# Newton-Schulz pseudo-inverse: block-diagonal 128x128 operands replaced by pairs of 64x64 products on quarter tiles

## The chip, the cores and the metric

The kernel runs on one core of a Trainium2 chip. The core has five engines that run side by side and meet at semaphores: PE (TensorE, matrix products; its weight loads are shown apart as PEld), DVE (VectorE), ACT (ScalarE), POOL (GpSimd) and SP (SyncE, here only a DMA queue). The metric is the device time of one execution in microseconds.

## What is computed

The input x has 8 batches of 2048 tokens with 256 features. The reference applies two residual blocks. The first is a Nyström attention with 16 heads of 16 features and 64 landmarks a head:

```python
q_l = q.reshape(B, H, M, denom, HS).sum(axis=-2) / denom
k_l = k.reshape(B, H, M, denom, HS).sum(axis=-2) / denom
s1 = jax.nn.softmax(jnp.einsum('bhld,bhmd->bhlm', q, k_l), axis=-1)
s2 = jax.nn.softmax(jnp.einsum('bhmd,bhnd->bhmn', q_l, k_l), axis=-1)
s3 = jax.nn.softmax(jnp.einsum('bhmd,bhld->bhml', q_l, k), axis=-1)
z_star = moore_penrose_pinv(s2, ITERS)
out = s1 @ (z_star @ (s3 @ v))
```

and the pseudo-inverse of each 64x64 matrix s2 is six steps of

```python
z = jnp.swapaxes(x, -1, -2) / (col * row)[..., None, None]
for _ in range(num_iter):
    xz = x @ z
    z = 0.25 * z @ (13.0 * I - xz @ (15.0 * I - xz @ (7.0 * I - xz)))
```

The second block is a gated feed-forward layer with a shift by one token. Both are wrapped in layer norms.

## The kernel before

The program has two parts. **Part 1** makes, for every batch, the layer-norm statistics of all tokens, the landmarks, the matrices s2 and their inverses; it stores landmarks and inverses to DRAM. It takes the eight batches in two groups of four (`for i in range(B // GR)`); the four of a group are called rows, `for s in ROWS`. **Part 2** does everything else, batch by batch, in an order written out by hand (the lists PRO, BODY, LAST); it begins when Part 1 has ended on all engines.

Inside a group of Part 1 each engine's program is a list of steps, and each step runs over the four rows before the next step begins. An engine works strictly in the order of its own program. So when DVE or ACT has a step that takes long, everything behind it in that engine's list waits, even where its operand is ready. The order in a group is: DMA of x1in (three buffers, so the fourth row's load waits until PE has pooled the first row), statistics on DVE (`st`, `mv`, L878 and L883), `pw` (L871), pooling on PE (L1188), landmarks, logits, softmax X (L912 to L926), its transpose XT by PE (L1166), then column sums and the split of XT ("cs, XTlo, XTbd", L945, L931, L940), the scale factor, and the six iterations.

**Numbers.** The products of the inverse are done in f16 with operands split in a high and a low half: a tile with `_d` in its name holds [128 partitions, 8 pairs of heads, 2 halves, 64]. The high half is written by ACT (`high`, L673), the low half by DVE (`low`, L931), both reading the product from PSUM. A product of two split operands takes three matmuls: high x high, high x low, low x high.

**Tiling.** Two heads share the 128 partitions: head 0 of a pair is on partitions 0 to 63, head 1 on 64 to 127. So that one matmul of the full array multiplies both heads without mixing them, the stationary operand is a block-diagonal copy, `_bd`, of [128, 8, 2, 128]: the two heads' 64x64 matrices stand on the diagonal and zeros elsewhere. The zeros are filled in once by POOL at the start of the program (L577, twelve fills). The blocks are copied in by DVE for XT and for S and T3 (`blocks`, L940, two copies a row and step) and by ACT for Z transposed (L687, two copies a row and iteration). `product` (L1172 to L1180) issues the matmuls, all at L1179: for each pair `a` the terms, each with a 128x128 stationary and a 64-column moving operand.

**An iteration.** S = X Z (24 matmuls a row), T2 = 15 I - 7 S + S S (48: the identity and the terms in S go through the array as well, against scaled identities eye15 and eye7), T3 = 13 I - S T2 (32), and last Z' = Z T3 and its transpose (24 each; the last iteration makes the transpose alone). Each of a group's four rows has two PSUM banks, named bank, wide, wide and acc. PE's step for row s waits for DVE's low half (or block copy) of row s; ACT's `high` waits for PE's product, DVE's `low` for ACT's `high`. ACT's copies into ZT_bd stand in its order between the high halves of S and those of T2.

Of the kernel before, what the change touches and what calls it, by code (L numbers as in the profile page):

```python
# [11 lines left out]
P = 128  # L12
# [3 lines left out]
def sandwich(nc, x, Wk, Wq, Wv, Wo, bo, W_r, W_k, W_v, mu_r, mu_k, out):  # L16
# [23 lines left out]
    with ctx:  # L40
# [3 lines left out]
        def sem(name):  # L44
            return ctx.enter_context(nc.semaphore(name))
# [82 lines left out]
        XT_bd = [sb(f"XT_bd{s}", [P, PAIRS, 2, P], F16, c=part1) for s in ROWS]  # L128
        ST_d = [sb(f"ST_d{s}", [P, PAIRS, 2, M], F16, c=part1) for s in ROWS]
        ST_bd = [sb(f"ST_bd{s}", [P, PAIRS, 2, P], F16, c=part1) for s in ROWS]  # L130
        Z_d = [sb(f"Z_d{s}", [P, PAIRS, 2, M], F16, c=part1) for s in ROWS]
        ZT_d = [sb(f"ZT_d{s}", [P, PAIRS, 2, M], F16, c=part1) for s in ROWS]
        ZT_bd = [sb(f"ZT_bd{s}", [P, PAIRS, 2, P], F16, c=part1) for s in ROWS]
# [6 lines left out]
        p_zero = sem("p_zero")  # L140
# [12 lines left out]
                      for s in ROWS for n in names]  # L153
                     + [(n, i, s) for i in range(ITERS) for names in (["S"], ["ZTbd"], ["T2"], ["T3"], ["Z", "ZT"])
                        for s in ROWS for n in names
                        if not (n in ("Z", "ZT", "ZTbd") and i == ITERS - 1)])
# [5 lines left out]
                                           ["max", "shift"], ["sum", "rcp", "X", "rs"], ["cs", "XTlo", "XTbd"],  # L162
                                           ["cm", "cg", "cr", "gb"], ["gcol", "gX", "gXT"], ["Zlo", "ZTlo"])
                      for s in ROWS for n in names]
                     + [(n, i, s) for i in range(ITERS)
                        for names in (["Slo", "Sbd"], ["T2lo"], ["T3lo", "T3bd"], ["Zlo", "ZTlo"])
# [376 lines left out]
        def _(pool):  # L543
# [84 lines left out]
        def _(act):  # L628
# [10 lines left out]
            for i in range(B // GR):  # L639
# [20 lines left out]
                for s in ROWS:  # L660
# [3 lines left out]
                    sc.activation(ST_d[s][:, :, 0, :], XT[s][:, :, :], ACT.Copy, scale=XS).then_inc(p_act, 1)  # L664
# [901 lines left out]
```

## Time and profile before

| | us |
|---|---|
| median of three runs | 2051.49 (2047.1 to 2055.32) |
| the profiled execution | 2045.3 |
| its span, first to last instruction | 2043.6 |
| PE busy | 1669.9 (82%) |
| DVE busy | 1428.1 (70%) |
| ACT busy | 990.2 (48%) |
| POOL busy | 268.8 (13%) |

The mean granted clock of TensorE over the span is 0.93 of its full 2.4 GHz. It has two levels, 1.2 and 2.4 GHz, shown as 0.50 and 1.00. The part of the time that Part 1 takes is read from the timeline: group 1 runs to 281.9 us, group 2 to 534.6. A busy time is an average over parts with different limits, so what a change in one stage is worth has to be read from that stage.

### The profile page before, as it was taken

How to read it: one execution, taken by the hardware profiler on the slowest of the kernel's cores; microseconds unless marked ns; L12 is line 12 of the kernel's file. 1: busy time of each engine (PE TensorE's matmuls, PEld its weight loads, DVE VectorE, ACT ScalarE, POOL GpSimd, SP SyncE). 2: the span in 40 equal slices, each digit the busy share in tenths (PEclk: the TensorE clock that was granted, in tenths of full speed). 3: DMA queues.
4: the chain of work that ended last, by engine and by line, in shares of the span. 5: the costliest groups of instructions: out<-in, count | busy, mean ns of one | idle time of the engine just before them, and what ended most of it. 6: DMA issues, size and time to landing. Idle time of an engine off the chain costs nothing.

```text
span 2043.6 us, 51115 instructions
## 1 busy us (share of the span) xinstructions
PE 1669.9 (82%) x21644; PEld 1141.4 (56%) x21644; DVE 1428.1 (70%) x3036; ACT 990.2 (48%) x1615; POOL 268.8 (13%) x134
## 2 busy tenths in 40 slices
PE   2758767687477988998898899889889988988885
PEld 1557755577345545655654655465456556556554
DVE  8487784877773688379468837956883794788265
ACT  1147721577223544654554465355446535543652
POOL 4000000000300111112111101211111121112022
PEclk9869988699787999999999999999999999999997
DMA  5230001000122121212212121221213122221110
GB/s 162 74 103 3 4 22 52 2 3 3 54 50 53 46 63 42 84 38 52 76 46 62 42 80 42 52 75 47 63 41 94 27 52 76 64 53 39 43 32 31
DMA packets 125700, 104.66 MB, mean 51 GB/s; under 512 B 30368, under 2 KB 123424, under 8 KB 125472
## 3 DMA queue, kind: packets, MB, share of 16 engines
q1 hardware_dynamic: 124320, 99.29, 17.8%
q8 instruction: 172, 2.82, 0.6%
q10 hardware_dynamic: 1152, 2.10, 0.3%
q14 instruction: 56, 0.46, 0.1%
HBM read 56.23 MB, written 19.92 MB: 37 GB/s over the span
## 4 chain that ended last, share of the span: by engine, by line
PE 49%; DVE 30%; issue 10%; ACT 8%; POOL 2%; DMA 1%; DVEq 0%; POOLq 0%; ACTq 0%; SPq 0%
PE bank L1491 5%; PE bank L1283 4%; DVE m L1035 4%; ACT ZT_bd L687 4%; PE bank L1470 4%; PE acc L1366 4%; PE bank L1511 3%; PE bank L1294 3%; PE acc L1283 3%; PE bank L1533 3%; DVE m L1027 3%; PE wide L1388 3%; DVE ST_d L931 2%; DVE ST_bd L940 2%; PE wide L1451 2%
## 5 line engine op out<-in xcount | busy, mean ns | idle before, releaser
L605 POOL TENSOR_TENSOR xm<-yy,xres 128x1024 f32<-128x1024 f32 x32 | 91.8, 2869 | 591.9 <-issue 339.3
L772 ACT ACTIVATE p<-wide 128x1024 f32<-128x1024 f32 x128 | 123.9, 1020 | 78.7 <-PE wide L1451 78.7
L743 ACT ACTIVATE e<-wide 128x1024 f32<-128x1024 f32 x128 | 130.0, 1022 | 63.9 <-PE wide L1388 58.9
L1035 DVE TENSOR_REDUCE m<-wide 128x16 f32<-128x1024 f32 x128 | 149.8, 1212 | 15.6 <-PE wide L1330 15.6
L1027 DVE TENSOR_REDUCE m<-wide 128x2 f32<-128x1024 f32 x128 | 149.3, 1215 | 10.0 <-PE wide L1310 10.0
L1533 PE MATMUL bank<-wvT,ka 128*128 128x256 f32 x512 | 133.7, 420 | 4.9 <-ACT ka L818 4.3
L1511 PE MATMUL bank<-wrT,xrT 128*128 128x256 f32 x512 | 124.3, 398 | 11.0 <-DVE ob L1121 6.4
L1491 PE MATMUL bank<-wo,oT 128*128 128x256 f32 x512 | 120.1, 388 | 4.5 <-DVE oT L1070 2.6
L621 POOL TENSOR_TENSOR ob<-ob,xm 128x1024 f32<-128x1024 f32 x32 | 76.5, 2390 | 355.7 <-DVE ob L273 355.7
L1533 PEld LDWEIGHTS bank<-wvT,ka 128*128 128x128 f32 x512 | 105.4, 211 | 30.2 <-issue 8.2
L1511 PEld LDWEIGHTS bank<-wrT,xrT 128*128 128x128 f32 x512 | 98.6, 198 | 31.1 <-issue 10.3
L1491 PEld LDWEIGHTS bank<-wo,oT 128*128 128x128 f32 x512 | 96.0, 192 | 27.2 <-issue 12.2
L1283 PE MATMUL bank<-xT,w 128*128 128x512 f16 x384 | 97.0, 406 | 7.7 <-DVE xT L1008 4.8
L1521 PE MATMUL acc<-xkT,wkT 128*128 128x512 f32 x192 | 88.3, 603 | 16.2 <-DVE oT L1070 16.2
L615 POOL TENSOR_TENSOR xkT<-x2T 128x1024 f32<-128x1024 f32 x32 | 60.6, 1892 | 309.8 <-ACT x2T L797 309.8
L1057 DVE RECIPROCAL rr<-bank 128x4 f32<-128x4 f32 x16 | 2.8, 183 | 138.6 <-PE bank L1401 138.5
L1294 PE MATMUL bank<-w,xT 128*128 128x256 f16 x768 | 89.2, 273 | 12.6 <-DVE ql L1016 12.6
L1366 PE MATMUL acc<-e,vv 128*17 128x64 f32 x4096 | 85.0, 223 | 16.8 <-issue 8.4
L1470 PE MATMUL bank<-p,ones_pair 128*32 128x512 f32 x512 | 85.5, 651 | 10.0 <-ACT p L772 10.0
L1294 PEld LDWEIGHTS bank<-w,xT 128*128 128x128 f16 x768 | 74.3, 98 | 30.3 <-DVE ql L1016 18.1
L1283 PE MATMUL acc<-xT,w 128*128 128x512 f16 x384 | 88.8, 381 | 0.0
L940 DVE COPY ST_bd<-ST_d 64x1024 f16<-64x1024 f16 x192 | 80.9, 422 | 11.1
(285 smaller groups left out, 3916.6 us busy)
## 6 DMA issues: line engine op xcount, KB each, us to landing
x1in<-in_L_attn_x SPq DMA_DIRECT2D x8, 2048.0 KB, 13.6
xin<-in_L_attn_x SPq DMA_DIRECT2D x32, 512.0 KB, 4.9
k_stack<-kh SPq DMA_DIRECT2D x256, 64.0 KB, 2.2
xres<-in_L_attn_x SPq DMA_DIRECT2D x32, 512.0 KB, 4.4
out<-ob SPq DMA_DIRECT2D x32, 512.0 KB, 2.9
k_stack<-kl SPq DMA_DIRECT2D x128, 64.0 KB, 2.0
q_stack<-landmarks SPq DMA_DIRECT2D x192, 4.0 KB, 1.6
inverse<-X ACTq DMA_DIRECT2D x8, 256.0 KB, 2.2
```

Source lines behind the costliest of these rows:

```text
L743: sc.activation(e3[t % 2][:, :], wide[t % 2][:, :], ACT.Exp).then_inc(wide_drained[t % 2], 1)
L772: sc.activation(p1[:, 2 * j:2 * j + 2, :], wide[w][:, :].rearrange("p (a n) -> p a n", a=2), ACT.Exp).then_inc(wide_drained[w], 1)
L940: ins = v.tensor_copy(dst[r, :, :, j * M:(j + 1) * M], src[r, :, :, :])
L1027: v.tensor_reduce(m3[:, 2 * j:2 * j + 2, c], wide[j % 2][:, :].rearrange("p (a n) -> p a n", a=2), AX.X, ALU.max).then_inc(wide_drained[j ...
L1035: v.tensor_reduce(m1[:, tiles, 2 * w:2 * w + 2, :].rearrange("p t q x -> p q t x"), wide[w][:, :].rearrange("p (q t x m) -> p q t x m", q= ...
L1283: ins = mm(dst[o][:, :], w16[:, w, wt, k, o * P:(o + 1) * P], xT[:, xt, k, :], start=(i == 0), stop=(i == len(TERMS) - 1))
L1294: ins = mm(bank[j][:, t * A:(t + 1) * A], xT[:, xt, k, tok], w16[:, 2, wt, k, :], start=(i == 0), stop=(i == len(TERMS) - 1))
L1366: ins = mm(acc[k][32 * q:32 * q + HS + 1, j * M:(j + 1) * M], vv[:, t, h, :], e3[t % 2][:, h * M:(h + 1) * M], start=(first and j == 0), s ...
L1470: s_ = mm(bank[k][r, :], ones_pair[:, :], p1[:, a, :], start=True, stop=True)
L1491: ins = mm(dst, oT[:, k, tok], wo[:, k, :], start=(k == 0), stop=(k == KB - 1))
L1511: ins = mm(bank[j][:, t * A:(t + 1) * A], xrT[:, k, tok], wrT[:, k, :], start=(k == 0), stop=(k == KB - 1))
L1533: ins = mm(bank[j][:, t * A:(t + 1) * A], ka[:, k, tok], wvT[:, k, :], start=(k == 0), stop=(k == KB - 1))
```

## The change

Each head's product is done by itself on a quarter of the array: the stationary and the moving operand are 64 partitions x 64 columns, rows 0 to 63 go to the upper left quarter and rows 64 to 127 to the lower right one, and the two quarters alternate, term by term. The operands are now the `_d` tiles themselves. The tiles XT_bd, ST_bd and ZT_bd, the copies into them on DVE and ACT, and POOL's fills are gone. Since S must now outlive the making of T2 (it is read as an operand from its `_d` tile), T2 gets a tile of its own, T2_d, and XT gets XT_d instead of a turn in ST_d. PE's two waits for the end of ACT and DVE between Part 1 and Part 2 are gone too.

```diff
             def product(dst, left, right, added=()):
 
+                halves = [slice(j * HALF, (j + 1) * HALF) for j in range(2)]
                 for a in range(PAIRS):
-                    terms = [(scaled(a), identity) for scaled, identity in added]
-                    terms += [(left[:, a, 0, :], right[:, a, 0, :]), (left[:, a, 0, :], right[:, a, 1, :]),
-                              (left[:, a, 1, :], right[:, a, 0, :])]
-                    for n, (l, r) in enumerate(terms):
-                        ins = mm(dst[:, a * M:(a + 1) * M], l, r, start=(n == 0), stop=(n == len(terms) - 1))
+                    terms = [[(scaled(r, a), identity[r, :]) for scaled, identity in added]
+                             + [(left[r, a, 0, :], right[r, a, 0, :]), (left[r, a, 0, :], right[r, a, 1, :]),
+                                (left[r, a, 1, :], right[r, a, 0, :])] for r in halves]
+                    last = len(terms[0]) - 1
+                    for n in range(last + 1):
+                        for j, r in enumerate(halves):
+                            ins = mm(dst[r, a * M:(a + 1) * M], *terms[j][n], start=(n == 0), stop=(n == last))
                 return ins
...
-            for s in ROWS:
-                for t in (XT_bd, ST_bd, ZT_bd):
-                    g.memset(t[s][:, :, :, :], 0.0).then_inc(p_zero, 1)
...
-                    if it < ITERS - 1:
-                        for s in ROWS:
-                            if it == 0:
-                                act.wait_ge(p_dve, of(dve_steps, i, "ZTlo", s))
-                            else:
-                                act.wait_ge(p_dve, of(dve_steps, i, "ZTlo", it - 1, s))
-                            act.wait_ge(p_zero, 3 * GR)
-                            for j in range(2):
-                                r = slice(j * HALF, (j + 1) * HALF)
-                                ins = sc.activation(ZT_bd[s][r, :, :, j * M:(j + 1) * M], ZT_d[s][r, :, :, :], ACT.Copy)
-                            ins.then_inc(p_act, 1)
                     for s in ROWS:
-                        high("T2", it, s, ST_d, pb[s][1], -1.0 / SS)
+                        high("T2", it, s, T2_d, pb[s][1], -1.0 / SS)
...
-                    low(("XThi", s), ST_d[s], XT[s][:, :, :], XS)
-                    blocks(("XTlo", s), XT_bd[s], ST_d[s])
+                    low(("XThi", s), XT_d[s], XT[s][:, :, :], XS)
...
                         low(("S", it, s), ST_d[s], pm(pb[s][0]), SS / (XS * ZS))
-                        blocks(("Slo", it, s), ST_bd[s], ST_d[s])
                     for s in ROWS:
-                        low(("T2", it, s), ST_d[s], pm(pb[s][1]), -1.0 / SS)
+                        low(("T2", it, s), T2_d[s], pm(pb[s][1]), -1.0 / SS)
                     for s in ROWS:
                         low(("T3", it, s), ST_d[s], pm(pb[s][0]), 1.0 / SS)
-                        blocks(("T3lo", it, s), ST_bd[s], ST_d[s])
...
-            pe.wait_ge(p_act, len(act_steps) * B // GR)
-            pe.wait_ge(p_dve, len(dve_steps) * B // GR)
```

The order on PE, where the first iteration of a group begins (S of the four rows, then T2 of row 0's first pair). Before:

```order
L1179 MATMUL bank0<-Z_d0,XT_bd0 128x64 x24
L1179 MATMUL wide0<-Z_d1,XT_bd1 128x64 x24
L1179 MATMUL wide1<-Z_d2,XT_bd2 128x64 x24
L1179 MATMUL acc0<-Z_d3,XT_bd3 128x64 x24
L1179 MATMUL bank1<-eye15,ident16 128x64
L1179 MATMUL bank1<-eye7,ST_bd0 128x64 x2
L1179 MATMUL bank1<-ST_d0,ST_bd0 128x64 x3
```

and after:

```order
L1153 MATMUL bank0<-Z_d0,XT_d0 64x64 x48
L1153 MATMUL wide0<-Z_d1,XT_d1 64x64 x48
L1153 MATMUL wide1<-Z_d2,XT_d2 64x64 x48
L1153 MATMUL acc0<-Z_d3,XT_d3 64x64 x48
L1153 MATMUL bank1<-eye15,ident16 64x64 x2
L1153 MATMUL bank1<-eye7,ST_d0 64x64 x4
L1153 MATMUL bank1<-ST_d0 64x64 x6
```

The steps stand in the same order; each has twice the matmuls of half the height.

The order on ACT in an iteration, from the high halves of S on. Before:

```order
L673 ACTIVATE ST_d<-bank 128x8x64
L673 ACTIVATE ST_d<-wide 128x8x64 x2
L673 ACTIVATE ST_d<-acc 128x8x64
L687 ACTIVATE ZT_bd<-ZT_d 64x16x64 x8
L673 ACTIVATE ST_d<-bank 128x8x64
L673 ACTIVATE ST_d<-wide 128x8x64 x2
L673 ACTIVATE ST_d<-acc 128x8x64
```

and after:

```order
L667 ACTIVATE ST_d<-bank 128x8x64
L667 ACTIVATE ST_d<-wide 128x8x64 x2
L667 ACTIVATE ST_d<-acc 128x8x64
L667 ACTIVATE T_d<-bank 128x8x64
L667 ACTIVATE T_d<-wide 128x8x64 x2
L667 ACTIVATE T_d<-acc 128x8x64
```

The eight copies between S and T2 are gone, and T2's halves go to their own tile (T_d is T2_d with its number left out).

The order on DVE for the low halves of S, after the eight pieces of Z and ZT. Before:

```order
L931 SCALAR_TENSOR_TENSOR ST_d<-bank,ST_d 128x8x64
L940 COPY ST_bd<-ST_d 64x16x64 x2
L931 SCALAR_TENSOR_TENSOR ST_d<-wide,ST_d 128x8x64
L940 COPY ST_bd<-ST_d 64x16x64 x2
L931 SCALAR_TENSOR_TENSOR ST_d<-wide,ST_d 128x8x64
L940 COPY ST_bd<-ST_d 64x16x64 x2
L931 SCALAR_TENSOR_TENSOR ST_d<-acc,ST_d 128x8x64
L940 COPY ST_bd<-ST_d 64x16x64 x2
```

and after, with the first of T2's:

```order
L914 SCALAR_TENSOR_TENSOR ST_d<-bank,ST_d 128x8x64
L914 SCALAR_TENSOR_TENSOR ST_d<-wide,ST_d 128x8x64 x2
L914 SCALAR_TENSOR_TENSOR ST_d<-acc,ST_d 128x8x64
L914 SCALAR_TENSOR_TENSOR T_d<-bank,T_d 128x8x64
L914 SCALAR_TENSOR_TENSOR T_d<-wide,T_d 128x8x64 x2
```

The copies of T3 and of XT go in the same way.

## Rows read from the trace of the kernel before

**Rows 1.** The page: the chain that ended last, by engine and line.

```profile
PE bank L1491 5%; PE bank L1283 4%; DVE m L1035 4%; ACT ZT_bd L687 4%; PE bank L1470 4%; PE acc L1366 4%; PE bank L1511 3%; PE bank L1294 3%; PE acc L1283 3%; PE bank L1533 3%; DVE m L1027 3%; PE wide L1388 3%; DVE ST_d L931 2%; DVE ST_bd L940 2%; PE wide L1451 2%
```

**Rows 2.** Windows, both groups' iterations: length, PE, PEld, DVE, ACT, POOL busy (count), clock.

```profile
130.20:282.00 151.80, 120.01 (x3552) 114.48 (x3552) 120.58 (x223) 109.00 (x155) 0.00 (x0) 0.93 0.02 6
383.60:534.70 151.10, 119.97 (x3552) 114.37 (x3552) 119.83 (x221) 108.48 (x154) 0.00 (x0) 0.93 0.02 6
```

**Rows 3.** The chain of waits from 172 to 199, by line.

```profile
by line: ACT ZT_bd L687 31.4%; PE wide L1179 12.2%; DVE ST_d L931 10.1%; DVE Z_d L931 9.2%; DVE ZT_d L931 8.8%; PE bank L1179 8.5%; DVE ST_bd L940 6.3%; issue 6.0%; ACT ST_d L673 4.5%; PE acc L1179 3.9%; ACT Z_d L673 2.2%; DVEq L862 0.2%
```

**Rows 4.** Timeline of DVE and ACT, 182 to 199: start, us, instruction, [idle before].

```profile
182.13 0.69 DVE L931 SCALAR_TENSOR_TENSOR Z_d<-bank,Z_d 128x512 f16<-128x512 f32 x1
182.74 0.68 DVE L931 SCALAR_TENSOR_TENSOR ZT_d<-bank,ZT_d 128x512 f16<-128x512 f32 x1
...
188.60 8.56 ACT L687 ACTIVATE ZT_bd<-ZT_d 64x1024 f16<-64x1024 f16 x8
...
197.81 0.69 DVE L931 SCALAR_TENSOR_TENSOR ST_d<-bank,ST_d 128x512 f16<-128x512 f32 x1 [4.20 <-ACT ST_d L673]
```

**Rows 5.** Timeline of PE, warm and cold, and the window of the cold one.

```profile
179.61 0.86 PE L1179 MATMUL bank<-ZT_d,ST_bd 128*128 128x64 f16 x24
...
133.47 2.75 PE L1179 MATMUL wide<-Z_d,XT_bd 128*128 128x64 f16 x48
...
134.00:137.00 3.00, 3.00 (x61) 3.00 (x59) 2.88 (x6) 1.49 (x3) 0.00 (x0) 0.50 0.02 5
```

**Rows 6.** Timeline of PE on f32 operands (stationary size first), and windows there.

```profile
107.30 1.97 PE L1166 MATMUL wide<-ident,X 64*64 64x64 f32 x32 [0.30 <-DVE X L922]
...
1023.73 3.19 PE L1417 MATMUL bank<-un,zt 64*64 64x16 f32 x32
...
92.96 1.95 PE L1209 MATMUL bank<-qlT,qbd 128*128 128x64 f32 x16
...
52.55 7.07 PE L1188 MATMUL wide<-x1in,pw 128*64 128x256 f32 x32
...
107.30:109.30 2.00, 1.97 (x32) 1.78 (x32) 1.93 (x4) 0.96 (x2) 0.00 (x0) 0.50 1.09 348
1023.70:1027.00 3.30, 3.30 (x40) 3.22 (x40) 1.33 (x5) 2.13 (x4) 0.00 (x0) 0.50 0.08 11
92.00:96.00 4.00, 4.00 (x39) 4.00 (x37) 1.62 (x4) 1.13 (x4) 0.00 (x0) 1.00 0.19 61
```

**Rows 7.** Timeline, first and last pieces around group 1's iterations.

```profile
130.86 0.68 DVE L931 SCALAR_TENSOR_TENSOR Z_d<-XT,Z_d 128x512 f16<-128x512 f32 x1
...
281.24 0.68 DVE L985 TENSOR_SCALAR X<-acc 128x512 f32<-128x512 f32 x1
```

**Rows 8.** Timeline of DVE, one row of "cs, XTlo, XTbd" to the next.

```profile
112.34 0.68 DVE L945 TENSOR_REDUCE rc<-XT 128x8 f32<-128x512 f32 x1
...
114.61 0.69 DVE L945 TENSOR_REDUCE rc<-XT 128x8 f32<-128x512 f32 x1
```

**Rows 9.** Timeline of POOL, DVE and ACT at the start, and a window.

```profile
3.47 1.80 POOL L577 MEMSET XT_bd<- 128x2048 f16 x1
...
3.56 21.00 DVE L841 CAST ident<-ident 128x128 f16<-128x128 f32 x1 [3.56 <-POOL eye L573]
...
25.25 0.68 DVE L854 SCALAR_TENSOR_TENSOR w<-wq,w 128x512 f16<-128x512 f32 x1
...
29.45 5.32 DVE L878 BATCH_NORM_STATS2 st<-x1in 128x6 f32<-128x256 f32 x16
...
15.72 0.62 ACT L638 ACTIVATE w<-wq 128x512 f16<-128x512 f32 x1
...
30.00:35.00 5.00, 0.00 (x0) 0.00 (x0) 4.86 (x16) 0.00 (x0) 0.00 (x0) 1.00 0.00 0
```

**Rows 10.** Timeline of PE in Part 2 and its window.

```profile
651.04 0.64 PE L1366 MATMUL acc<-e,vv 128*17 128x64 f32 x32
...
650.00:652.00 2.00, 2.00 (x79) 1.63 (x72) 0.00 (x0) 1.90 (x2) 0.00 (x0) 1.00 0.03 8
```

More of the change, by code:

```diff
@@ L127, in sandwich @@
         XS, ZS, SS = 64.0, 16.0, 16.0
-        XT_bd = [sb(f"XT_bd{s}", [P, PAIRS, 2, P], F16, c=part1) for s in ROWS]
+        XT_d = [sb(f"XT_d{s}", [P, PAIRS, 2, M], F16, c=part1) for s in ROWS]
         ST_d = [sb(f"ST_d{s}", [P, PAIRS, 2, M], F16, c=part1) for s in ROWS]
-        ST_bd = [sb(f"ST_bd{s}", [P, PAIRS, 2, P], F16, c=part1) for s in ROWS]
+        T2_d = [sb(f"T2_d{s}", [P, PAIRS, 2, M], F16, c=part1) for s in ROWS]
         Z_d = [sb(f"Z_d{s}", [P, PAIRS, 2, M], F16, c=part1) for s in ROWS]
         ZT_d = [sb(f"ZT_d{s}", [P, PAIRS, 2, M], F16, c=part1) for s in ROWS]
-        ZT_bd = [sb(f"ZT_bd{s}", [P, PAIRS, 2, P], F16, c=part1) for s in ROWS]
         pb = [[bank[0][:, :], bank[1][:, :]], [wide[0][:, 0:512], wide[0][:, 512:1024]],
@@ L153, in sandwich @@
                       for s in ROWS for n in names]
-                     + [(n, i, s) for i in range(ITERS) for names in (["S"], ["ZTbd"], ["T2"], ["T3"], ["Z", "ZT"])
+                     + [(n, i, s) for i in range(ITERS) for names in (["S"], ["T2"], ["T3"], ["Z", "ZT"])
                         for s in ROWS for n in names
-                        if not (n in ("Z", "ZT", "ZTbd") and i == ITERS - 1)])
+                        if not (n in ("Z", "ZT") and i == ITERS - 1)])
         STATS = ([("st", 0), ("st", 1)] + [k for s in range(2, GR) for k in (("pw", s - 2), ("st", s))]
@@ L161, in sandwich @@
                      + [(n, s) for names in (["stl", "mvl", "xl"], ["lmlo", "qbd"],
-                                           ["max", "shift"], ["sum", "rcp", "X", "rs"], ["cs", "XTlo", "XTbd"],
+                                           ["max", "shift"], ["sum", "rcp", "X", "rs"], ["cs", "XTlo"],
                                            ["cm", "cg", "cr", "gb"], ["gcol", "gX", "gXT"], ["Zlo", "ZTlo"])
@@ L932, in low @@
                                            op0=ALU.mult, op1=ALU.subtract).then_inc(p_dve, 1)
-                def blocks(lo_key, dst, src):
-                    dve.wait_ge(p_zero, 3 * GR)
-                    done(*lo_key)
-                    for j in range(2):
-                        r = slice(j * HALF, (j + 1) * HALF)
-                        ins = v.tensor_copy(dst[r, :, :, j * M:(j + 1) * M], src[r, :, :, :])
-                    ins.then_inc(p_dve, 1)
                 for s in ROWS:
@@ L1230, in _ @@
                         pe.wait_ge(p_dve, of(dve_steps, i, *key))
-                        product(pb[s][0], XT_bd[s], Z_d[s]).then_inc(p_pe, 1)
+                        product(pb[s][0], XT_d[s], Z_d[s]).then_inc(p_pe, 1)
                     for s in ROWS:
-                        pe.wait_ge(p_dve, of(dve_steps, i, "Sbd", it, s))
-                        product(pb[s][1], ST_bd[s], ST_d[s],
-                                [(lambda a: ident16[:, :], eye15[:, :]),
-                                 (lambda a: ST_bd[s][:, a, 0, :], eye7[:, :]),
-                                 (lambda a: ST_bd[s][:, a, 1, :], eye7[:, :])]).then_inc(p_pe, 1)
+                        pe.wait_ge(p_dve, of(dve_steps, i, "Slo", it, s))
+                        S_ = ST_d[s]
+                        product(pb[s][1], S_, S_, [(lambda r, a: ident16[r, r], eye15),
+                                                   (lambda r, a: S_[r, a, 0, :], eye7),
+                                                   (lambda r, a: S_[r, a, 1, :], eye7)]).then_inc(p_pe, 1)
                     for s in ROWS:
                         pe.wait_ge(p_dve, of(dve_steps, i, "T2lo", it, s))
-                        product(pb[s][0], ST_bd[s], ST_d[s],
-                                [(lambda a: ident16[:, :], eye13[:, :])]).then_inc(p_pe, 1)
+                        product(pb[s][0], ST_d[s], T2_d[s], [(lambda r, a: ident16[r, r], eye13)]).then_inc(p_pe, 1)
                     for s in ROWS:
-                        pe.wait_ge(p_dve, of(dve_steps, i, "T3bd", it, s))
+                        pe.wait_ge(p_dve, of(dve_steps, i, "T3lo", it, s))
                         if it < ITERS - 1:
-                            pe.wait_ge(p_act, of(act_steps, i, "ZTbd", it, s))
-                            product(pb[s][1], ZT_bd[s], ST_d[s]).then_inc(p_pe, 1)
-                        product(pb[s][0], ST_bd[s], ZT_d[s]).then_inc(p_pe, 1)
-            pe.wait_ge(p_act, len(act_steps) * B // GR)
-            pe.wait_ge(p_dve, len(dve_steps) * B // GR)
+                            product(pb[s][1], ZT_d[s], ST_d[s]).then_inc(p_pe, 1)
+                        product(pb[s][0], ST_d[s], ZT_d[s]).then_inc(p_pe, 1)
             pe.wait_ge(w16_lo, 3)
```

5 lines of the change are left out of this document (2 added, 3 removed).

## The prediction

> **What bounds the kernel now.** I read the page's chain of waits first: PE's lines lead it, but DVE's and ACT's block-diagonal copies stand among its largest entries, DVE ST_bd and ACT ZT_bd [rows 1]. All of them lie in two stretches, the six iterations of the inverse for batches 0 to 3 and for 4 to 7, so I read those alone: 151.8 and 151.1 us, with PE, DVE and ACT each busy for 109 to 120 us of them [rows 2]. No engine is full; the stage goes in turns. The chain of one iteration says whose turn is longest: ACT's copies into ZT_bd hold 31% of it, DVE's into ST_bd 6% [rows 3]. The timeline shows how: ACT starts eight copies at 188.60 and works on them for 8.56 us. The evacuation of T2 stands behind them in ACT's order, so DVE has nothing to read until 197.81, after 4.20 us of idleness [rows 4]. PE waits behind DVE. A full iteration comes to about 25 us, a sixth of the stage.
>
> The stage's work on PE is 3552 products a group: a row of the batch needs 24 (XZ) + 48 (T2) + 32 (T3) + 24 + 24 (Z and its transpose) = 152, four rows 608, five iterations of that, and a last one without Z of 512; the count in the windows agrees [rows 2]. A product is one load and one matmul of 64 columns. 24 of them take 0.86 us, of which the last one's own latency is 0.193, so one starts every 29.0 to 29.2 ns while the clock is at the upper level, 2.4 GHz; at the lower level, 1.2 GHz, 48 take 2.75 us, 53 ns each [rows 5]. 3552 x 0.0292 = 103.7 us: that is the floor under the stage's 151, and 47 us are turns.
>
> **The change, part by part.**
>
> *Copies of ACT and DVE.* Gone are 40 ACT copies a group, and 48 pairs of DVE copies of 0.86 us inside the iterations. What stays of each engine in a full iteration is 20 evacuations at 0.60 us pitch (the pitch of DVE's pieces in [rows 4]; ACT's pieces are as long), 12 us for either. PE's part is above 17, so PE becomes the bound if its turns close. They do: after XZ of the last row the first T2 needs one ACT and one DVE piece, 1.5 us with latencies, while PE still has three rows of XZ, 3 x 0.7 us; DVE's eight Z pieces, 4.8 us, fit under PE's Z and ZT products, 5.6 us. Every later step has longer rows and the same two pieces. So the stage is PE's product count times the pace of a quarter-tile pair.
>
> *The pace of a pair.* Each product becomes two, one in the upper left and one in the lower right quarter, each with its own load of 64 columns. The instructions double to 7104 loads and 7104 matmuls a group. Are two quarters worked on at once? The trace has both cases, with f32 operands. The transposes of X alternate the two quarters: 32 matmuls in 1.97 us, of which 0.31 is latency, 53.5 ns each at the lower clock. The product of un and zt walks through one quarter first and then the other: 32 in 3.19 us at the same clock, 94 ns each, with the same load of 64 columns and a shorter matmul [rows 6]. A load in one quarter and one in the other thus run side by side, and a pair of the first kind takes 107 ns, the time of one load.
>
> What does a load of 64 f16 columns take at the upper clock? For f32, 128 columns are loaded in 111.7 ns ((1.95 - 0.275)/15), with matmuls of 64 columns behind them that would need only 54 by the 216 ns of 256 columns ((7.07 - 0.38)/31). So the load sets this pace: 106.7 ns, two cycles a column, and 5 on top [rows 6]. f16 matmul columns cost half of f32 ones: 29.2 for 64 against 216 for 256. I take the same half for the load: 64 columns in 26.7 ns, and with the 5 on top a pair every 31.7 ns. Bounds: from below the 29.2 of today (a matmul of 64 columns cannot stream faster); from above the load at f32's two cycles, 53.3 + 5 = 58.3 ns. I stand near the lower end because the rows show that the matmul side halves, and the load is the same stream of columns.
>
> The Trainium skill speaks against this change here: "TensorEngine Tiling (Array Packing)", section Restrictions, says that column tiling disables Fast Weight Load. The 128-column f16 loads have it, the 64-column ones would not. "TensorE: Matmul & The Clock Gate", section LDWEIGHTS, gives such a load as its columns over 1.2, which is 53.3 ns for 64; by that estimate the pair would take 53 to 58 ns and the sum would be that of the first rival. The trace's f32 loads agree with this formula (106.7 for 128); for f16 no row shows it.
>
> Sum of the stage: 3552 x 0.0317 = 112.6 us. In front stand 1.3 us (DVE's first two pieces from 130.86 on [rows 7], 0.60 + 0.68). The clock is at the lower level until about 137 [rows 5]: 5 us in which 94 pairs pass instead of 158, 2.0 us lost. Behind the last product stands one DVE piece, 0.8 us. Together 116.7, against 281.92 - 130.86 = 151.1 now [rows 7]. That saves 34.4 a group, **68.8 us** for two. PE then has no idle stretch in the stage, so I count no second fall of the clock.
>
> *Copies into XT_bd.* A row of "cs, XTlo, XTbd" takes DVE 2.27 us (112.34 to 114.61) on the chain, of which 0.60 + 0.60 remain [rows 8]. 4 rows x 1.07 x 2 groups = **8.6 us**. ACT's pieces for the last row do not take their place: the transposes of row 1 start at 107.30 [rows 6], those of row 3 two turns of 2.27 later, at 111.8, and with 2.0 for them and 0.6 + 0.6 for ACT are over at 115.1; DVE's new pace gets to that row at 115.9. Bounds: 7 if ACT's last piece holds DVE a little, 9 if not.
>
> *The fills on POOL.* Twelve fills of 1.80 us run from 3.47 on. DVE's cast of ident, 128 columns, is issued at 3.56 and lasts 21.00 us, until the last fill is over [rows 9], where 512 columns take DVE 0.69 [rows 4]. Without the fills DVE is through with its constants by 6 at the latest and waits for ACT's f16 weights, which start at 15.72 and give the first at 16.4. From the first weight piece (25.25) to the first statistics (29.45) are 4.2 us, so these start at 20.6: **8.8 us** sooner. x1in is no new wait: the three first loads are all in before 30, as the window with no traffic shows, and DVE now reaches the third at 33.8. Pooling, the fourth load and all that follows hang on this chain. Bounds 0 (should the cast wait for something else) and 9.
>
> The Trainium skill gives the reason for the long cast ("SBUF — State Buffer", Who interferes with whom): a DVE copy or cast in a two-port mode and a GpSimd instruction exclude each other. By it the cast is short again once the fills are gone; the trace agrees, with 21.00 us beside them.
>
> *The rest.* PE's final waits on ACT and DVE go: its next instruction waits for xhat from DVE, which itself waits for both, nothing. T2_d costs nothing; each evacuation writes as many bytes as before. Part 2 is only moved earlier.
>
> Sum: 68.8 + 8.6 + 8.8 = 86.2. The profiled execution took 2045.3 us (span 2043.6) and would take 1959. The median of the runs is 2051.5, 6 above it; from there I predict **1965 us**. A measurement of this kernel can tell some 0.5%, 10 us, from no change.
>
> **The rivals.**
>
> *Slow loads (slower than before).* The f16 load of 64 columns goes at f32's pace, 58.3 ns a pair: 3552 x 0.0583 = 207.1, 94.5 more than in my sum, 189 for two groups: 2154 us. For it: no row shows an f16 load under 128 columns. Against: the halving above. It turns from gain to loss at 31.7 + 86.2/(2 x 3.552) = 43.8 ns a pair.
>
> *Lower clock (slower).* Half of the array stands still in these matmuls, and the chip might grant only 1.2 GHz: 53.3 ns a pair, 189.3 a group, 74.7 more after the 2.0 already counted, 2115 us. Against: around 651, with 17-column matmuls for half of the time, the clock stays at 1.00 [rows 10].
>
> *Delivery.* PE must take four instructions per pair, one every 7.9 ns, for 100 us without a pause. Bursts do it: 32 matmuls and 32 loads in 0.64 us of which 0.22 is latency, 6.8 ns an instruction [rows 10]. Over longer stretches the trace shows less: 79 + 72 in 2.00 us in the same place, 13 ns each, which the work there sets. At 10 ns an instruction a pair takes 40: 142.1 a group, 2 x 29.5 more, 2024 us, still a gain.
>
> *It does not do what it says:* quarters taken one after the other, 63 ns a pair, over 2180. The transposes speak against it.
>
> **How the numbers follow.** My forecast 0.72, delivery 0.06, slow loads 0.14, lower clock 0.06, the rest 0.02. The forecast's own range: 29.2 instead of 31.7 ns takes 18 off, an earlier rise of the clock 4 and the spread of the runs 4, 1940; 36 ns adds 31 and a lost start 9, 2005. To hold 8 in 10 the range takes in delivery and ends at 2030. Faster: forecast and delivery, 0.78; within 0.5%: 0.02; slower: slow loads, clock and the rest, 0.20.
>
> **What the profile after would show.** Each group's stage at some 117 us with PE busy nearly throughout; the products of a row of Z, 48 matmuls now, in 0.76 us plus latency (0.70 at 29.2, 1.4 for the rival); DVE and ACT idle for a third of an iteration; the granted clock at 1.00 from the first iteration on; DVE's cast at 3.6 lasting under 1 us and the first statistics at 20.6. I am wrong if the pair takes over 36 ns, if the clock falls inside the stage, or if PE shows waits between the steps.

## The result and the profile after

The changed kernel takes **2134.9 us** (median of 4 runs, 2131.9 to 2140.3) against 2049.3 for the kernel before in the same runs: 1.042 of its time, with a 95% interval of 1.038 to 1.046. I had predicted 1965, with a range of 1940 to 2030. The change is a loss of 4%, where I forecast a gain of 4%.

The page of the profiled execution (2140.3 us, span 2138.5) already names what is new. These are its two lines on the chain that ended last, by engine and by line:

```profile
PE 57%; DVE 20%; issue 15%; ACT 3%; POOL 2%; DMA 1%; SPq 0%; POOLq 0%; DVEq 0%; ACTq 0%
PE wide L1153 6%; PE bank L1459 4%; PE bank L1251 4%; DVE m L1006 3%; PE bank L1438 3%; PE acc L1334 3%; PE bank L1501 3%; PE bank L1479 3%; PE bank L1262 3%; PE acc L1153 3%; PE bank L1153 3%; PE acc L1251 3%; PE wide L1356 3%; DVE m L998 3%; PE wide L1419 2%
```

ACT's ZT_bd and DVE's ST_bd [rows 1] are gone from it, as they should be. In their place stands "issue", 15% of the span where it had 10: time in which an engine waits for nothing that the profile shows. Where it lies, the windows of the two groups' iterations tell, the rows that answer to [rows 2] (length, then PE, PEld, DVE, ACT, POOL busy and count, then granted clock, DMA share, GB/s):

```profile
117.50:321.00 203.50, 131.44 (x7104) 125.32 (x7104) 82.75 (x121) 66.86 (x112) 0.00 (x0) 0.94 0.03 7
418.20:621.90 203.70, 129.80 (x7104) 124.10 (x7104) 82.61 (x121) 66.86 (x112) 0.00 (x0) 0.95 0.02 6
```

From its first product to its last a group took 147.9 us before and takes 203.5 now. DVE fell from 120 to 83 us of work and ACT from 109 to 67, and the clock is at 0.94. PE is busy for 131 of 203.5 us: it is neither full nor, as before, waiting for a copy. The chain in the middle of the stage, 164 to 175.4, shows what it does in the other 72 (its line by line, then start, us, what):

```profile
by line: issue 43.6%; PE acc L1153 20.8%; PE bank L1153 19.6%; PE wide L1153 19.4%
...
163.74 1.24 issue
164.98 1.36 PE acc L1153 x74
166.34 0.85 PE bank L1153 x54
167.19 1.24 issue
168.44 0.34 PE bank L1153 x10
168.78 1.87 PE wide L1153 x118
170.65 1.24 issue
```

No other engine is on this chain, nor on that of the whole stage from 118 to 320, where "issue" is 72 us:

```profile
by line: issue 35.5%; PE wide L1153 32.5%; PE acc L1153 16.7%; PE bank L1153 15.4%
```

PE works for 2.2 us, stands still for 1.24, works again, in a period of 3.45 us. Between two idle pieces stand 74 + 54 = 128 matmuls, and then 10 + 118 = 128 again: with their loads, 256 instructions. And while it works it is as fast as forecast: 118 matmuls in 1.87 us, 15.8 ns each, 31.7 for a pair of quarters. The transfers of the stage carry the other half of the explanation. These are the rows of queue 8, which brings instructions (packets, MB, share of 16 engines), of the changed kernel from 118 to 320, and of the kernel before from 130 to 282:

```profile
q8 instruction: 55, 0.90, 1.8%
```

```profile
q8 instruction: 28, 0.46, 1.3%
```

55 packets of 16 KB in 202 us, one every 3.67 us, for 14208 loads and matmuls a group: 258 to a packet. PE's instructions arrive in blocks of some 256, and it uses a block up in 2.2 us where the next comes 3.45 to 3.7 us after the last. The kernel before took 28 blocks in 152 us, one every 5.4.

The start and end of each packet, as the trace records them, fit the pauses. Packets end at 163.76, 167.09, 170.40 and 173.81, and PE goes on at 164.98, 168.44, 171.89 and 175.34, each time 1.2 to 1.5 us after one is in. In none of the traces of this case do two packets of queue 8 start less than 3.2 us apart.

The kernel before, which has no product of this kind, shows such a pause too. In Part 2 its packets start at 1361.74, 1365.15 and 1368.69 and the next only at 1374.56; that one ends at 1375.49. PE goes on at 1377.00. Its chain from 1373 to 1381 has this piece:

```profile
1375.31 1.69 issue
```

So such a pause comes without quarter tiles. Whether it is what sets the length of the stage, the experiments ask.

### The profile page after: what moved, and what is told of

Its sections match the earlier page's. It is cut to its first block, busy times and chain, and to the rows that moved or that the text cites. A ratio compares the mean times of both kernels' runs of the same rounds, so it can differ in the third digit from the quotient of the medians.

```text
span 2138.5 us, 64838 instructions
## 1 busy us (share of the span) xinstructions
PE 1693.1 (79%) x28748; PEld 1161.2 (54%) x28748; DVE 1329.2 (62%) x2828; ACT 908.9 (42%) x1535; POOL 247.8 (12%) x122
## 4 chain that ended last, share of the span: by engine, by line
PE 57%; DVE 20%; issue 15%; ACT 3%; POOL 2%; DMA 1%; SPq 0%; POOLq 0%; DVEq 0%; ACTq 0%
PE wide L1153 6%; PE bank L1459 4%; PE bank L1251 4%; DVE m L1006 3%; PE bank L1438 3%; PE acc L1334 3%; PE bank L1501 3%; PE bank L1479 3%; PE bank L1262 3%; PE acc L1153 3%; PE bank L1153 3%; PE acc L1251 3%; PE wide L1356 3%; DVE m L998 3%; PE wide L1419 2%
## 5 line engine op out<-in xcount | busy, mean ns | idle before, releaser
L1041 DVE TENSOR_TENSOR oT<-acc,oT 128x512 f32<-128x512 f32 x64 | 42.3, 681 | 67.8 <-ACT oT L766 67.7
```

## The experiments

Two theories. **Supply:** PE's instructions come in at no more than 256 per 3.45 to 3.7 us, some 14 ns each, and the stage lasts as long as its instructions take to arrive, whatever the array does. **Quarters:** the stalls belong to the work on quarter tiles itself, and 128 such matmuls cost one.

### Fewer instructions, the same array work

```diff
+                if whole is not None:
+                    mm(dst.rearrange("p (a m) -> p a m", m=M), ident16[:, :],
+                       whole[:, :].unsqueeze(1).to_broadcast([P, PAIRS, M]), start=True, stop=False)
...
-                        product(pb[s][0], ST_d[s], T2_d[s], [(lambda r, a: ident16[r, r], eye13)]).then_inc(p_pe, 1)
+                        product(pb[s][0], ST_d[s], T2_d[s], (), eye13).then_inc(p_pe, 1)
```

> The changed kernel, with one edit: the identity term of T2 and of T3 (16 times the identity against 15 or 13 times it), eight pairs of quarter-tile products a row, becomes one product of the whole array with 512 columns. The array gets about the same work (8 pairs at 32 ns = 256 ns before, one of 512 columns at some 216 ns now), but 30 instructions fewer for each such step, 60 a row and iteration: 14208 PE loads and matmuls a group become 12768. Theory 1 (PE's instructions arrive at no more than one per 14.3 ns, 256 every 3.67 us): the stage falls with the count, 204 to 183 us a group, 41 us for both, to about 2094 us. Theory 2 (the stalls belong to the quarter tiles or to the pace of the array): at most the 2 x 48 x 0.04 = 4 us of array time go, about 2131 us.

Measured: 2104.6 us, 1.025 of before (1.021 to 1.029), 30 less than the changed kernel. The first group's window:

```profile
117.00:297.00 180.00, 133.25 (x6384) 115.49 (x6384) 83.11 (x122) 67.03 (x113) 0.00 (x0) 0.97 0.03 8
```

179.6 us from first to last product, 24 less. The second group took 187.5; the stages of 14208 instructions vary as much between groups and kernels, 196 to 206 us. Per instruction that is 179.6 / 12768 = 14.1 ns, against 203.5 / 14208 = 14.3. The array's busy time rose by 2 us while the stage fell by 24: this is supply's answer. The 4 us that I expected of the other theory were too few by its own terms: 768 quarter matmuls fewer a group are also six stalls fewer, some 8 us a group, so it asked for about 2115 us and a stage near 194. The run is outside that too. The time in which PE stood still fell from 72 to 46 us in the group, where six stalls are 8. The control is the same edit on the kernel before:

> The kernel before, with the identity terms of T2 and of T3 as one product of 512 columns each: 28 instructions fewer a row and iteration, the array's work the same to within 2%. It is the control of the same edit on the changed kernel, which gained 24 us in the first group. Theory 1 (instruction supply bounds only a stage that asks for more than 256 in 3.67 us): before, the products take 29.2 ns, 128 of them 3.74 us, so supply does not bound and the groups stay at 147.9 us from first to last product, the time within 0.3%. If the edit itself is cheaper for the array, the groups fall here as well, by up to 24 us each.

Measured: 2051.6 us, 1.001 (0.999 to 1.003), and a group as long as before, 148.3 us from first to last product:

```profile
130.00:279.00 149.00, 121.06 (x3216) 108.36 (x3216) 117.45 (x217) 107.80 (x153) 0.00 (x0) 0.92 0.01 3
```

The edit is worth nothing where supply doesn't bind.

### Less array work, the same instructions

```diff
-                            ins = mm(dst[r, a * M:(a + 1) * M], *terms[j][n], start=(n == 0), stop=(n == last))
+                            l, m = terms[j][n]
+                            ins = mm(dst[j * HALF:j * HALF + 32, a * M:a * M + 32], l[:, 0:32], m[:, 0:32],
+                                     start=(n == 0), stop=(n == last))
```

> The changed kernel with every product of the iterations cut to 32 of its 64 output rows and 32 of its 64 columns, the rest of each inverse left out: a load of 32 columns and a matmul of 32 columns in place of 64 and 64, so the array has half the work per instruction, and the instructions are as many as before, 14208 a group. Theory 1 (supply: 256 instructions in 3.67 us): nothing is gained, 204 us a group, 2135 us in all, with the runs between the idle pieces shorter and the idle pieces longer. Theory 2 (the array's pace on quarters): a pair takes about 16 to 20 ns in place of 32, and the stage falls towards the 12 us an iteration that the evacuations need, under 120 us a group, below 1970 us.

Measured: 2134.9 us, the changed kernel's time to the tenth. Its window, the chain from 160 to 182 by line, and queue 8 from 118 to 314:

```profile
118.00:314.00 196.00, 104.82 (x7094) 98.73 (x7095) 80.74 (x122) 66.96 (x113) 0.00 (x0) 0.51 0.03 8
```

```profile
by line: issue 45.2%; PE wide L1154 33.0%; PE bank L1154 11.3%; PE acc L1154 10.5%
```

```profile
q8 instruction: 55, 0.90, 1.9%
```

The array has half the columns to load and half to stream, PE's busy time falls by 27 us, and the stage by 7. (Even that 7 need not be the edit's: the stage of the changed kernel itself, unedited but for fills on POOL, took 199.5 and 197.8 us in the run with the fills put back, below.) Even the clock doesn't matter: it is granted at 0.51 here, the lower level, against 0.94, and the time is the same. The idle pieces are longer, 1.57 to 1.84 us, where PE needs less for a block; stalls of a fixed length would have made the stage 105 + 72 = 177 us. Again 55 blocks of instructions, now in 196 us. This is the cleanest of the runs: the array is not what the stage waits for.

### Two runs meant for the same question that answered another

A kernel with one quarter alone:

```diff
-                        for j, r in enumerate(halves):
+                        for j, r in list(enumerate(halves))[:1]:
```

> The changed kernel with the lower right quarter of every product of the iterations left out, so half of the heads get no inverse: 7104 loads and matmuls a group instead of 14208, all in one quarter, so nothing of them runs side by side. Theory 1 (instruction supply): a load and matmul in one and the same quarter come every 31.7 ns by my forecast, slower than the supply's 2 x 14.3 = 28.6 ns, so the long idle pieces of PE put down to issue vanish, and each group takes about 117 us: 2049 - 14.7 x 2 (what the changed kernel gains in front of the iterations is 14.7 and 5) ... in short about 1963 us. Theory 2 (a stall of 1.2 to 1.8 us belongs to every 128 quarter matmuls): 28 stalls of 1.4 us stay in each group, about 155 us, 2040 us in all. A quarter's load taking 53 ns would show as a pitch of 58 ns and 207 us a group.

Measured: 2113.5 us, 1.029 (1.024 to 1.034). Its window, and two pieces of its chain:

```profile
116.00:306.00 190.00, 189.65 (x3552) 189.51 (x3552) 83.14 (x123) 67.06 (x113) 0.00 (x0) 0.50 0.02 5
```

```profile
139.95 1.28 PE bank L1153 x24
141.23 5.12 PE wide L1153 x96
```

The stalls are gone, as supply has it: 128 matmuls take 6.8 us here and the next block is in long before. The other theory wanted 28 stalls in 3552 quarter matmuls, and no two instructions of PE start more than 0.06 us apart in the 190. But both theories missed the time, since neither reckoned with the clock: PE is busy for all of the 190 us, and the granted clock stays at 0.50, 1.2 GHz. A matmul comes every 5.12 / 96 = 53.3 ns. 3552 x 0.0533 = 189.4 is the whole group. My rival "lower clock" had this number for the full kernel; it holds for a single quarter alone.

Waits added on PE in the kernel before:

```diff
                     for n, (l, r) in enumerate(terms):
+                        pe.wait_ge(eyes_made, 4)
+                        pe.wait_ge(const_made, NCONST)
```

> The kernel before, with its full-array products and its copies, and two more wait instructions on PE ahead of each product's load, on conditions long met: 4 instructions per product, 14208 a group, as many as the changed kernel has, and the array's work is unchanged. Theory 1 (instruction supply): each group's iterations go from 151 to about 204 us, idle pieces put down to issue come up in them about every 64 products, and the whole takes about 2156 us. Theory 2 (the stalls belong to quarter tiles): the waits cost at most the few ns that PE's sequencer needs for each, hidden under the 29 ns of a product, and the time stays within 1% of the kernel before.

Measured: 2695.4 us, 1.31. Neither expectation, 2156 us or within 1%, came near: a wait on a condition long met isn't free on PE. A row of the timeline, and the window from 140 to 250:

```profile
140.63 1.56 PE L1181 MATMUL acc<-Z_d,XT_bd 128*128 128x64 f16 x11
```

```profile
140.00:250.00 110.00, 109.21 (x828) 85.89 (x827) 25.73 (x45) 31.71 (x41) 0.00 (x0) 0.50 0.01 1
```

828 products in 110 us, 133 ns each, where 53 is the pace of a product at this same lower clock: two waits cost some 80 ns, and no idle piece comes up. The instructions don't come thick enough to ask anything of the supply, so this run tells nothing between the theories.

### The order of the quarters

```diff
-                    for n in range(last + 1):
-                        for j, r in enumerate(halves):
+                    for j, r in enumerate(halves):
+                        for n in range(last + 1):
```

> The changed kernel, each pair's terms ordered otherwise: all terms of the upper left quarter, then all of the lower right one. Same instructions, same count. Theory 1 (instruction supply, and a load is hidden only under a matmul of the other quarter): products of one quarter come every 31.7 ns, 128 of them take 4.06 us, more than the 3.67 us in which 256 instructions arrive, so the idle pieces put down to issue nearly vanish and PE's own pace sets the stage: 7104 x 0.0317 = 225 us plus 4, 24 more than the changed kernel a group, 2183 us. If the order of the quarters does not matter to the array, the pitch stays at 16 ns and the time at 2135 us. Theory 2 (stalls belong to the quarters): both add up, 225 + 55 stalls of 1.4 us, over 2300 us.

Measured: 2141.6 us, 1.043 (1.038 to 1.048), the same as the changed kernel. Its window shows the same stalls, and the same pace between them:

```profile
117.00:321.00 204.00, 127.58 (x7100) 122.08 (x7094) 82.90 (x122) 66.86 (x112) 0.00 (x0) 0.97 0.03 8
```

The times of the two theories, 2183 us and over 2300, didn't come; what did is the case that the expectation had set beside them, in which the order doesn't matter to the array. Three to six terms of one quarter in a row are no slower than quarters in turn, so the run tells nothing between the theories. It looks as if PE begins work of the other quarter from several instructions ahead; that is my interpretation, no row shows it. Whether there is an end to it, the next kernel asks, with 24 to 48 of one quarter in a row:

```diff
-                for a in range(PAIRS):
+                for j in range(2):
+                    r = slice(j * HALF, (j + 1) * HALF)
+                    for a in range(PAIRS):
```

> The changed kernel, each product of a row ordered otherwise: all eight pairs of the upper left quarter (24 to 48 matmuls in a row), then all eight of the lower right one. Same instructions, 14208 a group. With three to six of a quarter in a row the stage took 203.7 us and a matmul came every 16 ns between the idle pieces, as with quarters in turn. Theory A (work of the two quarters runs side by side only as far as the engine looks ahead, and 24 are beyond that): each comes every 31.7 ns at the upper clock, 128 in 4.06 us against 3.67 us of supply, so 7104 x 0.0317 = 225 us a group and 2183 us in all; and should one quarter at a time keep the clock at its lower level, as in the kernel with one quarter alone, 53.3 ns each, 379 us a group and 2490 us in all. Theory B (the load and the matmul of one quarter overlap enough for 16 ns by themselves): supply stays the bound, 204 us a group and 2135 us in all.

Measured: 2404.9 us, 1.175 (1.170 to 1.179). The first group's window:

```profile
116.00:452.00 336.00, 333.12 (x7048) 333.12 (x7049) 85.15 (x126) 69.16 (x116) 0.00 (x0) 0.50 0.01 3
```

336 us a group with PE busy throughout and the clock at 0.50 to the end. It is theory A in its second form, a little better than its 379: 336 / 7104 = 47.3 ns a matmul, where 53.3 is the pace of one quarter at this clock, and the start times show where the difference lies: 53 to 54 ns apart inside one quarter's run, 26 to 28 for a few where the other quarter's begins. The order matters after all once the runs are long. How much of the 132 us is the order's and how much the clock's this run doesn't separate. The clock alone is not enough: in the changed kernel quarters in turn came every 26.7 ns at the lower clock (48 in 1.49 us, of which 0.24 is the last one's latency), and 7104 x 0.0267 = 190 us would still lie under the supply's 204.

```profile
117.50 1.49 PE L1153 MATMUL bank<-Z_d,XT_d 64*64 64x64 f16 x48 [6.22 <-DVE ZT_d L914]
```

### The fills at the start

```diff
+            for s in ROWS:
+                for t in range(3):
+                    if t:
+                        pool.wait_ge(p_zero, 3 * s + t)
+                    g.memset(filled[s][:, :, :, :], 0.0).then_inc(p_zero, 1)
```

> The changed kernel with twelve fills of 1.80 us put back on POOL at the place where they stood, into tiles that nothing reads. If the fills were what held DVE's first cast, the cast lasts 21 us again and the first statistics start at 29.4 in place of 20.14 us: 9.3 us slower, 2144 us. If the cast waited for something else that the change took away, the time stays at 2135 us.

Measured: 2134.4 us (1.036 to 1.046 of before). The 9.3 us didn't come, because the long cast didn't: the first statistics start at 19.83 here. So the run doesn't price the late start that it was made for. Yet the fills do hold the cast; it is the waits between them, needed because three fills now share one tile, that let it through. The cast and the first fills of this run; then the same cast where 8 fills follow each other without a wait (the kernel of the next section), and in the changed kernel without fills:

```profile
3.48 5.53 POOL L579 MEMSET filled<- 128x2048 f16 x3
3.57 1.79 DVE L832 CAST ident<-ident 128x128 f16<-128x128 f32 x1 [3.57 <-POOL eye L573]
```

```profile
3.56 14.01 DVE L829 CAST ident<-ident 128x128 f16<-128x128 f32 x1 [3.56 <-POOL eye L572]
```

```profile
3.56 0.23 DVE L824 CAST ident<-ident 128x128 f16<-128x128 f32 x1 [3.56 <-POOL eye L571]
...
20.14 5.33 DVE L861 BATCH_NORM_STATS2 st<-x1in 128x6 f32<-128x256 f32 x16
```

21.00 us behind 12 fills without waits [rows 9], 14.01 behind 8, 1.79 behind one, 0.23 with none: the cast waits for the fills that POOL starts back to back, 1.75 us each, and gets in at the first pause.

### Quarter tiles for one product only

Supply says where quarter tiles should pay: where they take a copy off the path, and the stage's instructions stay within what arrives. Of the three copies ACT's into ZT_bd is the dearest, 31% of the chain [rows 3], and the product that it serves is 24 of a row's 152.

```diff
-                            pe.wait_ge(p_act, of(act_steps, i, "ZTbd", it, s))
-                            product(pb[s][1], ZT_bd[s], ST_d[s]).then_inc(p_pe, 1)
+                            quarters(pb[s][1], ZT_d[s], ST_d[s]).then_inc(p_pe, 1)
```

Only PE's part is shown. ACT's copies into ZT_bd and POOL's four fills of it are gone as well.

> The kernel before, where only the product with ZT on its left (24 of 152 products of a row) goes to quarter tiles, which makes ACT's copies into ZT_bd and their fills needless; the copies into ST_bd and XT_bd stay. 2 x 24 instructions more for each row: 1408 for each of the first five iterations in place of 1216. Theory 1 (supply): 1408 instructions arrive in 20.2 us, about what DVE (20 pieces of 0.60 and 8 pairs of 0.86, 19 us) and PE (17.7 and a little) need, so an iteration falls from 25 to some 21 us and a group from 151 to about 131; with a start 6.6 us earlier (8 fills in place of 12 keep DVE's cast) this is 2050 - 40 - 7 = 2003 us. Theory 2 (quarter tiles carry the stalls, 1.4 us for each 128 matmuls): 192 quarter matmuls an iteration add 2.1 us, some 2023 us. A kernel faster than both would be the outcome of either.

Measured: **1997.9 us**, 0.976 of the kernel before (0.973 to 0.979), faster than both. Its two groups, and its chain from 160 to 200:

```profile
124.00:252.20 128.20, 117.77 (x4032) 111.75 (x4032) 117.41 (x217) 66.91 (x113) 0.00 (x0) 0.98 0.02 4
356.00:484.20 128.20, 118.11 (x4032) 111.98 (x4032) 117.40 (x217) 66.88 (x113) 0.00 (x0) 0.98 0.02 4
```

```profile
by line: DVE ST_bd L928 29.6%; DVE ST_d L919 22.8%; DVE Z_d L919 12.4%; DVE ZT_d L919 12.0%; PE acc L1167 11.7%; ACT ST_d L672 4.5%; issue 4.5%; PE bank L1167 2.4%; DVEq L850 0.7%
```

128 us a group, 3 under what was expected, with DVE and PE busy for 117 each. 8064 instructions at 14.3 ns are 115 us: supply is just inside, "issue" is 4.5%, and the chain is DVE's.

Two more edits on it, the identity terms as one product and the fills held back:

> The kernel of the run before this one in the list (ZT's product alone on quarter tiles), and two more edits: the identity terms of T2 and T3 are one product of 512 columns each, which takes 28 instructions a row and iteration away, and POOL's 8 fills wait until DVE's constants are made. Supply is then 1296 instructions an iteration, 18.6 us, under what DVE needs, so the iterations gain at most 1 us each over the run before; the start gains 2.4 us more, since no fill stands beside the cast: 2003 - 2 - 0 to 12 = 1989 to 2001 us. If the fills now hold DVE's weight pieces at 15.9 us instead, the start gains nothing.

Measured: 2006.7 us, 0.980 (0.977 to 0.983), above the 1989 to 2001 expected and 9 us behind the kernel that it builds on. The groups are the same, 127.9 us, but 12.7 us are lost between them (249.4 to 366.0, against 252.2 to 356.1), in the projections, where its clock was at the lower level for longer (one profiled execution of either). Windows over these, first of this kernel, then of the one before it:

```profile
300.00:336.00 36.00, 34.70 (x170) 31.50 (x168) 12.96 (x25) 6.23 (x19) 0.00 (x0) 0.64 0.05 15
```

```profile
300.00:322.00 22.00, 21.07 (x156) 17.79 (x154) 8.85 (x19) 4.34 (x16) 0.00 (x0) 1.00 0.08 25
```

170 matmuls in 36 us at 0.64 of the clock, against 156 in 22 us at 1.00. To see whether the earlier start brings that about, I let POOL pause between the fills of the kernel that has only ZT's product changed:

> The kernel with only ZT's product on quarter tiles (0.976 of the kernel before in its run), and one more edit: POOL waits for each of its 8 fills to be over before it starts the next. If DVE gets in between two fills whenever POOL waits (as in the run with twelve such fills, where the cast took 1.79 us), the cast lasts under 2 us in place of 14.01, the first statistics start at some 20 us in place of 22.46, and the time falls by 2.4 us to 0.975 of the kernel before. The run with the later fills had the same earlier start and lost 12.7 us between the groups, where the granted clock was at its lower level from 300 to 340 us: should that follow from the earlier start, it comes up here too, 0.980.

Measured: 1999.4 us, 0.976 (0.973 to 0.978). The cast takes 1.79 us and the first statistics start at 21.1 in place of 22.5, and nothing of that can be told in the total. The long stretch at the lower clock didn't come up, so the earlier start alone doesn't cause it; what does is open.

## Why the prediction was wrong, step by step

**What bounds the kernel before** was read rightly. Taking ACT's ZT_bd copies away, and nothing else of the copies, made a group 20 us shorter (148 to 128), its product now on quarters. That the turns close was right as well: with all copies gone only PE and its pauses are on the stage's chain.

**The pace of a pair** was right: 31.7 ns forecast, 31.7 measured (118 matmuls in 1.87 us). The start times show the two quarters side by side: the second one's matmul 3 to 4 ns behind the first one's, the next pair 28 to 29 ns later. That the number fits to the tenth is in part luck. The 26.7 ns for an f16 load came from rows on f32, and no run tells whether the load or the matmul sets the 31.7. The rival of slow loads is out: two loads and two matmuls pass in 31.7 ns. The Trainium skill's figure for such a load ("TensorE: Matmul & The Clock Gate", LDWEIGHTS: columns over 1.2) would by my estimate from it, 53.3 ns, have made a pair 53 ns at least. The trace doesn't agree: at the upper clock a pair took 31.7 ns.

**Copies into XT_bd and the start** were right. The first statistics start at 20.14 in place of 29.45 [rows 9], 9.3 us against 8.8. The row of "cs, XTlo" takes 1.19 us in place of 2.27 [rows 8]:

```profile
101.97 0.68 DVE L919 TENSOR_REDUCE rc<-XT 128x8 f32<-128x512 f32 x1
102.56 0.68 DVE L914 SCALAR_TENSOR_TENSOR XT_d<-XT,XT_d 128x512 f16<-128x512 f32 x1
103.16 0.68 DVE L919 TENSOR_REDUCE rc<-XT 128x8 f32<-128x512 f32 x1
```

Together the first group's iterations began 14.7 us sooner (DVE's first piece of Z at 116.16, before at 130.86 [rows 7]).

**The step that failed is delivery**, the price of an instruction that comes in. I named it, worked out that PE would have to take one every 7.9 ns for 100 us, and then gave it 10 ns and 6 in 100. The measured price is 14.3 ns: 57.3 for a pair, over the break-even of 43.8 that I had worked out myself. The 10 came from nowhere but a burst of 6.8 ns in 0.42 us [rows 10], 64 instructions, a quarter of one block: it says how fast PE takes what it already has, not how fast more comes. PE has more than one block in hand when it has stood still for a while: in the first group the first pause comes only after 877 instructions, at 127.08. The only longer row that I had, 79 and 72 in 2.00 us, says 13.2 ns. I set it aside as what "the work there sets". Taken as the price it gives 53 ns a pair, 3552 x 0.053 = 188 a group, 75 more than in my sum, 2115 us: a forecast of slower, within 1% of the result. That closeness would have been luck, for 151 instructions are less than one block and can't show what a block costs. The instruction packets would have warned as well. The densest stretch of the kernel before that I find now is from 1361 to 1378, and queue 8 has there

```profile
q8 instruction: 4, 0.07, 1.4%
```

one block in 4.2 us, where the change asked for one in 256 x 7.9 ns = 2.0. No two start less than 3.35 us apart in the whole trace, and PE's pause of 1.69 us lies in this very stretch.

With 203.6 in place of the 112.6 the sum closes. From the first product to the last the groups grew by 2 x 55.7 = 111.3 us; 14.7 less in front of the first; 7.6 less between them (384.9 - 280.1 = 104.8 before, 418.2 - 321.0 = 97.2 now); and 6.0 more behind the second (1516.6 against 1510.6), a part that no edit touches, and that came out between 1507 and 1521 in the kernels with the same code there. 111.3 - 14.7 - 7.6 + 6.0 = 95.0, and the profiled executions differ by 2140.3 - 2045.3 = 95.0.

**Lower clock:** not as the rival had it: 0.94 over the stage, though it fell for a while inside it (0.85 on average from 180 to 220), which the forecast had ruled out. Nor would it have cost the 74.7 us a group that I gave it: with the stage waiting for instructions, the run with half-size products took the same time at 0.51. But the rival was nearer than its 0.06: with one quarter alone, or with 24 and more of one quarter in a row, the clock stayed at 0.50 for the whole stage.

**What the profile would show:** PE busy throughout was wrong, and its waits were the sign to look for. The stage of 117 us and the clock at 1.00 throughout were wrong too, and DVE and ACT stand idle for 59% and 67% of the stage, not a third. The short cast, the first statistics (20.6 forecast, 20.14) and, between the pauses, the pace of a row's Z were right.

## What to carry to other kernels

Smaller tiles multiply PE's instructions, and those came in at a rate of their own here: before splitting matmuls, count loads and matmuls in the stage, multiply by 14 ns, and compare that with the stage's length. A burst of a hundred instructions says nothing on a stream of thousands. The mark of it are idle pieces of PE that no other engine explains, one for each 256 instructions, with a packet of queue 8 ending just before each of PE's starts. Where the product fits, use quarters only for the operand whose copy is on the path; here that was 24 products of 152, and it gave 2.4% where all of them cost 4.2%.

## What the runs showed of the hardware that I had not expected

- PE's instructions arrive in blocks of 16 KB, 256 of them, every 3.45 us where PE waits in the middle of the stage and every 3.67 on average over it: 14.3 ns for each. No two blocks start less than 3.2 us apart in any trace. Four kernels with 14208 loads and matmuls a group and nothing slower in their way (the changed one, and those with half-size products, with the terms of a quarter in a row, and with the fills put back) took 196 to 206 us for it, at a granted clock of 0.51 as at 0.97.
- With quarters in turn, or in runs of three to six, the granted clock was 0.94 to 0.97 over the stage and a matmul came every 16 ns between the pauses. With one quarter alone, or in runs of 24 to 48, PE was busy all the time and the clock 0.50, with 53.3 and 47.3 ns for each.
- Two met waits ahead of each product cost PE some 80 ns a product at the lower clock (133 ns for 53).
- Fills that POOL starts back to back hold a DVE cast until the last of them (14.01 us for 8, 21.00 for 12); with a wait between them the cast passes after one, in 1.79 us.
- One product of 512 columns of the whole array can open the sums that products of quarter tiles then add to (the run with fewer instructions).
